# Attention sort: GpSimd makes the smaller keys of the last step of each sort place

## The reference

```python
q_prime = relu(einsum('bhld,hdm->bhlm', q, proj))
k_prime = relu(einsum('bhld,hdm->bhlm', k, proj))
kv_cumsum = cumsum(einsum('bhlm,bhld->bhlmd', k_prime, v), axis=2)
context = einsum('bhlm,bhlmd->bhld', q_prime, kv_cumsum)
norm = einsum('bhlm,bhlm->bhl', q_prime, cumsum(k_prime, axis=2))
out = (context / (norm[..., None] + 1e-06)) @ out_w + out_b
...
router_scores = softmax(xt @ Wr + br, axis=-1)          # 4096 tokens x 64 experts
order = argsort(-router_scores, axis=0)
sorted_vals = take_along_axis(router_scores, order, axis=0)
group_score = sorted_vals.reshape(Tq, G, En).sum(axis=1)
```

## Time and profile before

| | us |
|---|---|
| median of 3 runs (968.47 to 975.49) | 969.58 |
| the profiled execution | 975.05 |
| its span | 973.3 |
| DVE busy in the span | 734.6 (75%) |
| PE busy | 811.6 (83%) |
| ACT busy | 442.0 (45%) |
| POOL busy | 210.5 (22%) |

### The profile page before, as it was taken

One profiled execution on the slowest core, in us unless ns is written; L12 is line 12 of the kernel. 1 busy time (PEld: TensorE's weight loads), 2 busy tenths in 40 slices (PEclk: granted clock), 3 DMA queues, 4 the chain that ended last, 5 costly groups with the idle time before them and its releaser, 6 DMA issues. The chain is left out here.

```text
span 973.3 us, 26710 instructions
## 1 busy us (share of the span) xinstructions
PE 811.6 (83%) x10846; PEld 460.9 (47%) x10846; DVE 734.6 (75%) x1384; ACT 442.0 (45%) x785; POOL 210.5 (22%) x174
## 2 busy tenths in 40 slices
PE   6588989989887747889988969999996986689985
PEld 3366766767675512334433423433442663355542
DVE  4625545888999969999786866888885457699984
ACT  3555656656655515556677812111112355323321
POOL 7050010100100120000016843433331000224240
PEclk9679999999999968999998999999998899899998
DMA  7400000000000003566838498888781000000001
GB/s 187 100 20 4 5 4 4 4 4 4 4 4 3 4 1 151 224 241 248 280 150 352 168 351 271 281 264 269 259 280 55 1 1 1 1 11 12 23 11 33
DMA packets 49700, 104.43 MB, mean 107 GB/s; under 512 B 9968, under 2 KB 24112, under 8 KB 49456
## 3 DMA queue, kind: packets, MB, share of 16 engines
q1 hardware_dynamic: 45360, 100.68, 29.9%
q10 hardware_dynamic: 4224, 2.10, 0.8%
HBM read 53.48 MB, written 48.23 MB: 105 GB/s over the span
## 5 line engine op out<-in xcount | busy, mean ns | idle before, releaser
L1308 PE MATMUL bank<-RS,Wd 128*128 128x512 f32 x256 | 132.2, 604 | 10.1 <-DVE RS L1371 9.5
L1371 DVE TENSOR_TENSOR RS<-so_ug,bank 128x512 f32<-128x512 f32 x128 | 84.2, 672 | 24.3 <-PE bank L1294 13.2
L974 ACT ACTIVATE att_qk<-bank 128x512 f32<-128x512 f32 x128 | 66.8, 602 | 56.0 <-PE bank L744 56.0
L1273 POOL TENSOR_TENSOR so_ug<-so_ug 128x512 f32<-128x512 f32 x48 | 63.0, 1313 | 108.9 <-DMA so_ug<-hidden 108.9
L1308 PEld LDWEIGHTS bank<-RS,Wd 128*128 128x128 f32 x256 | 46.7, 191 | 62.0 <-DVE RS L1371 31.7
L1614 POOL TENSOR_TENSOR so_made<-so_ug 128x512 f32<-128x512 f32 x23 | 35.6, 1563 | 160.4 <-DVE bank L1817 150.3
L1638 ACT ACTIVATE so_ug<-bank,bu 128x512 f32<-128x512 f32 x80 | 54.7, 683 | 18.5 <-PE bank L57 18.4
L1069 DVE TENSOR_TENSOR att_am<-bank,causal 128x512 f32<-128x512 f32 x32 | 22.0, 688 | 46.1 <-PE bank L781 46.1
L55 PE MATMUL bank<-Hhi,Wgh 128*128 128x512 f16 x128 | 49.4, 386 | 8.8 <-DVE so_made L1769 8.5
L1985 POOL TENSOR_TENSOR ff_xn_h<-ff_xn_h,la_qT 128x1408 f32<-128x1408 f32 x7 | 22.2, 3169 | 153.5 <-DVE ff_xn_h L99 153.5
L481 DVE TENSOR_TENSOR att_sorting<-att_sorting 128x256 f32<-128x256 f32 x103 | 49.8, 484 | 0.0
(11 more groups left out here) (421 smaller groups left out, 1932.1 us busy)
## 6 DMA issues: line engine op xcount, KB each, us to landing
so_ug<-hidden SPq DMA_DIRECT2D x48, 768.0 KB, 4.5
hidden<-so_off SPq DMA_DIRECT2D x48, 512.0 KB, 2.9
hidden<-so_made SPq DMA_DIRECT2D x80, 256.0 KB, 2.0
so_ug<-hidden SPq DMA_DIRECT2D x16, 512.0 KB, 4.2
prep_xin<-in_L_attn_x_dram ACTq DMA_DIRECT2D x8, 256.0 KB, 7.7
out_dram<-ff_ot SPq DMA_DIRECT2D x8, 256.0 KB, 2.2
so_other<-so_key SPq DMA_DIRECT2D x2, 512.0 KB, 5.6
prep_wm<-in_L_wmod_dram SPq DMA_DIRECT2D x2, 384.0 KB, 5.9
```

The lines of the kernel that those rows point to most:

```text
L974: nc.scalar.activation(qk[t % 2][:, r, :, :].rearrange("p a l -> p (a l)"), psF[r], ACT.Relu).then_inc(s_["fe"], 1)
L1273: nc.gpsimd.tensor_tensor(u, u, g, ALU.mult).then_inc(s_pp, 1)
L1308: nc.tensor.matmul(psY[j][:, :], Wd[:, n, :], hh[n % 4][:], start=False, stop=n == EBLK - 1).then_inc(s_dn[n % 4], 1)
L1371: nc.vector.tensor_tensor(hh[i][:], pg[four % 2][:, i if four % 2 else i // 2 * 3 + i % 2, :], psW[k % 4][:, :], ALU.mult).then_inc(s_hh[k ...
```

## The change

In each sort place whose last step is a plain one (not the first step of the sort, and not one that reads the second half backwards), VectorE keeps the `max` and no longer issues the `min`. GpSimd reads both input halves as int32, adds them into a new tile `att_both`, and then subtracts the larger keys that VectorE wrote: sum less larger is the smaller. The bits of the positive floats are taken as integers for that. The list `SHARED` holds these places: 43 of the 51 in chunks 13 to 26 and 29 to 31. The next sort step on VectorE now waits for GpSimd's subtraction (it does the step's increment of the `sort` semaphore), and the subtraction waits for VectorE's `max` (`greater`) and for GpSimd's own sum (`both`). On GpSimd the sort work is put between the router's and the residual's instructions in the order of VectorE's places.

```diff
+                if i == 0 and before is not None:
+                    dve.wait_ge(before, FIRST + len(SORT_LOCAL))
...
+                if greater is not None and i == last - 1:
+                    size = SORT_LOCAL[i][0]
+                    nc.vector.tensor_tensor(halves(dst, size)[0], *halves(src, size), ALU.max).then_inc(greater, 1)
+                else:
+                    compare_exchange(dst, src, *SORT_LOCAL[i]).then_inc(stepped, 1)
...
+                SHARED = []
+                for t, (a, first, n) in sorted(SORTS.items()):
+                    cut = [0, n // 4, n * 5 // 8, n]
+                    for part in range(3):
+                        i = first + cut[part + 1] - 1
+                        if cut[part + 1] > cut[part] and i > 0 and not SORT_LOCAL[i][1]:
+                            SHARED.append((t, part, a, i))
...
-                        for s in range(NU - 1):
-                            residual(s)
-                            rt.modulate(pool, s, s, ops=nc.gpsimd)
-                            rt.h_low(pool, s, s, ops=nc.gpsimd)
+                        def lesser(t, part):
...
+                                    pool.wait_ge(s_[f"sort{a}"], FIRST + i)
+                                    nc.gpsimd.tensor_tensor(total, first.bitcast(I32), second.bitcast(I32),
+                                                            ALU.add).then_inc(s_["both"], 1)
+                                    pool.wait_ge(s_["both"], FIRST + k + 1)
+                                    pool.wait_ge(s_["greater"], FIRST + k + 1)
+                                    nc.gpsimd.tensor_tensor(lower.bitcast(I32), total, upper.bitcast(I32),
+                                                            ALU.subtract).then_inc(s_[f"sort{a}"], 1)
+                        for t in range(4, NCH):
+                            s, ph = t // 4 - 1, t % 4
+                            if ph == 3:
+                                rt.modulate(pool, s, s, ops=nc.gpsimd)
+                            lesser(t, 0)
+                            if ph == 3:
+                                rt.h_low(pool, s, s, ops=nc.gpsimd)
+                            lesser(t, 1)
+                            if ph == 1:
+                                residual(s)
+                            lesser(t, 2)
```

More of the change, by code:

```diff
@@ L9 @@
 U32 = mybir.dt.uint32
+I32 = mybir.dt.int32
 ALU = mybir.AluOpType
@@ L484, in program, with sort_tiles, halves, sort_local @@
         HELD = 19
-        def sort_local(dve, a, stepped, base, pads, scores_in, first, last):
+        def sort_tiles(a, i, pads):
             held = HELD if a == 2 else None
             own = slice(a * SORTED_RUN, (a + 1) * SORTED_RUN)
+            src = RS[:, own] if i == 0 else keys[:, own] if i == held else pads[(i + 1) % 2][:]
+            dst = keys[:, own] if i + 1 in (len(SORT_LOCAL), held) else pads[i % 2][:]
+            return dst, src
+        def halves(tile, size):
+            h = tile.rearrange("p (n k) -> p n k", k=size)
+            return h[:, :, 0:size // 2], h[:, :, size // 2:size]
+        def sort_local(dve, a, stepped, base, pads, scores_in, first, last, greater=None, before=None):
             for i in range(first, last):
@@ L494, in sort_local @@
                 dve.wait_ge(stepped, base + i)
-                src = RS[:, own] if i == 0 else keys[:, own] if i == held else pads[(i + 1) % 2][:]
-                dst = keys[:, own] if i + 1 in (len(SORT_LOCAL), held) else pads[i % 2][:]
-                compare_exchange(dst, src, *SORT_LOCAL[i]).then_inc(stepped, 1)
+                if i == 0 and before is not None:
+                    dve.wait_ge(before, FIRST + len(SORT_LOCAL))
+                dst, src = sort_tiles(a, i, pads)
+                if greater is not None and i == last - 1:
[3 more added lines that the diff above has]
+                    compare_exchange(dst, src, *SORT_LOCAL[i]).then_inc(stepped, 1)
         class Router:
@@ L660, in causal_attention @@
                 names = ("f", "fe", "kt", "kte", "S0", "S1", "Sv0", "Sv1", "Ae", "Ao", "me", "mo", "O", "Od", "To", "den",
-                         "rd", "o2", "C", "cd", "Y", "yd", "xu", "qk", "qke", "v", "vd", "sort0", "sort1", "sort2",
+                         "rd", "o2", "C", "cd", "Y", "yd", "xu", "qk", "qke", "v", "vd", "sort0", "sort1", "sort2", "greater", "both",
                          "mg", "gates", "w1T", "w1", "wq", "wqd", "gu", "dn", "pw")
@@ L681, in causal_attention @@
                 MERGES = {27: (0, 5), 28: (5, 5)}
+                SHARED = []
[5 more added lines that the diff above has]
+                            SHARED.append((t, part, a, i))
+                both = tmp.enter_context(nc.sbuf_tensor("att_both", [P, SORTED_RUN // 2], I32))
                 stand(dma=list(s_load.values()))
@@ L713, in residual @@
                             nc.gpsimd.tensor_tensor(XT[:, cols], XT[:, cols], yt[:], ALU.add).then_inc(s_["xu"], 1)
-                        for s in range(NU - 1):
-                            residual(s)
-                            rt.modulate(pool, s, s, ops=nc.gpsimd)
-                            rt.h_low(pool, s, s, ops=nc.gpsimd)
+                        def lesser(t, part):
+                            for k, (at, p, a, i) in enumerate(SHARED):
+                                if (at, p) == (t, part):
+                                    dst, src = sort_tiles(a, i, pads)
+                                    size = SORT_LOCAL[i][0]
+                                    first, second = halves(src, size)
+                                    upper, lower = halves(dst, size)
+                                    total = both[:].rearrange("p (n k) -> p n k", k=size // 2)
+                                    pool.wait_ge(s_[f"sort{a}"], FIRST + i)
[16 more added lines that the diff above has]
+                            lesser(t, 2)
                     @block.tensor
@@ L1107, in sort @@
                                 sort_local(dve, a, s_[f"sort{a}"], FIRST, pads, (rt.done(2 * a + 1, "td"),),
-                                           first + cut[part], first + cut[part + 1])
+                                           first + cut[part], first + cut[part + 1],
+                                           s_["greater"] if any(x[:2] == (t, part) for x in SHARED) else None,
+                                           s_[f"sort{a - 1}"] if a > 0 else None)
                             if t in MERGES:
```

## The result

| | us |
|---|---|
| before, median of 20 runs (960.98 to 975.49) | 969.77 |
| changed, median of 20 runs (969.87 to 978.62) | 974.03 |
| ratio, with its 95% interval | 1.0055 (1.0035 to 1.0075) |
| the profiled execution of the changed kernel | 969.87 |
| its span | 967.9 |

The change costs time, 5.3 us by the ratio (3.4 to 7.3), which is under 1% and still clear of the spread of the runs. What the 43 `min` instructions less give back is smaller than what the new waits cost.

What follows compares the result with a forecast made beforehand. VectorE was taken to set the pace of nearly every chunk with sort work. Places +2.0, +12.3 and -2.8, TensorE slack -2.8 and GpSimd order +1.3 made +10.0 on the 969.58 us median: 979.6 us, range 969 to 1000.

Steps and rivals of the forecast that it cites:

- the wait sits in slack: Rival: GpSimd at 0.62 us and more chunks than 14 and 18 waiting for TensorE; +3, 973 us; chance 0.18.
- The size of GpSimd's instruction: Each of 86 GpSimd 128x256 int32 instructions: 0.73 us, from float32 add rows; bounds 0.62, 0.85 and 1.27 us.
- The new wait: From lone `max` to next sort step: `max`, sum behind it, 0.15 us, subtraction, 0.03 us; 1.91 us unless covered.
- The second places: Second sort place of a chunk, 15 shared: +12.3 us, of it +10.2 in nine with nothing behind them.
- The port: VectorE and GpSimd share an exclusive SBUF port lock, so the sum runs behind `max`; without it, some 3.5 us less.
- First places: First sort place of a chunk, 13 shared: +0.54 us in seven covered only by the division; together +2.0 us.
- Third places and slack: Third sort place, 15 shared: eleven gain 0.25 us, -2.8; slack behind TensorE in chunks 14 and 18, another -2.8.
- it is faster: Rival: GpSimd's pair wholly hidden, 14.6 us go less some 3 in chunks that TensorE bounds; 958 us; chance 0.04.
- GpSimd's order: Sort work queued behind residual and `h_low` on GpSimd: +1.3 us, a sixth of such a row in some seven places.

Runs made afterwards that it cites:

- second pair of traces: Kernel before and changed kernel, both unchanged, run once more for a second trace: 972.10 us and 971.22 us, one run each.
- GpSimd beside whole steps: Against the kernel before: VectorE makes whole steps, GpSimd its 86 instructions on unrelated tiles, no sort step waiting: 987.47 us, ratio 1.0224.
- a second `min`: Kernel before plus one more `min` of the same input, into a tile nobody reads, in the same 43 places: 980.44 us, ratio 1.0131.
- the free removal: The 43 `min` left out with nothing in their place, GpSimd making no smaller keys, against the kernel before: 965.65 us, ratio 0.9969.

## Why the prediction was right, and which of its terms were not

The forecast was 979.6 us, +10.0, with a range of 969 to 1000; measured are 974.03 us, +5.3 by the ratio (3.4 to 7.3). That is inside the range, on the side forecast but under the 1%, and at the lower edge of the band that the forecast gave itself (+5 to +17), two thirds of the way to the rival *the wait sits in slack* (+3). The forecast held slower by over 1% for a little likelier (0.51) than within 1% (0.45), and it came within; that a change under 1% can't be told from none did not hold with 20 runs of each kernel. Measured from the lone `max` to the next sort step in both traces, place by place, the sums are:

| places | forecast | from the traces | second pair of traces |
|---|---|---|---|
| first | +2.0 | +1.2 | +0.7 |
| second | +12.3 | +10.3 | +10.3 |
| third, with the wait for TensorE behind them | -2.8 - 2.8 | -7.4 | -6.3 |
| all | +8.7 | +4.1 | +4.7 |
| everything else in the stage | +1.3 | +1.4 | +1.5 |

(The third place of chunk 31 is left out, since its next sort step lies in another stage.)

- **The size of GpSimd's instruction** was right: 0.73 us worked out of the two float32 rows, 0.72 to 0.75 us in 41 of 43 subtractions, so neither the 0.62 nor the 0.85 of its bounds.
- **The new wait** was the mis-sized term: 1.91 us forecast, 1.75 or 1.85 measured. 0.15 us to the subtraction was taken from a row with another history; it is 0.08 in 39 of 43 places. And the sum ends 0.58 us behind the `max`, as reckoned, in one kind of place only, and 0.47 behind it where the halves are single columns or pairs. Over the nine second places with nothing in between the shorter chain makes 1.2 us, and the distance before, 0.80 us and not 0.78, another 0.1; over all second places the forecast is 2.0 us too high.
- **The second places** are what costs, as forecast: shown by the run with them alone (+7.3) and the one without them (+0.5).
- **The port** holds as forecast. That it costs time with no semaphore involved is shown by the run with GpSimd beside whole steps (+21.7).
- **First places.** Two of them (chunks 17 and 30) cost nothing, which the forecast missed. Their first place is a single step, and its input was ready well ahead: in chunk 30 because the third place of chunk 29 is not shared, in chunk 17 because VectorE waited for TensorE at `am` and at a state update (0.20 and 0.94 us). In the second trace chunk 18 does the same. The sum is then done by the time of the `max` (chunk 30, both engines):

```profile
323.36 0.73 POOL L750 TENSOR_TENSOR att_both<-att_sorting 128x256 int32<-128x256 int32 x1 [3.54 <-DVE att_sorting L482]
...
324.67 0.42 DVE L511 TENSOR_TENSOR att_sorting<-att_sorting 128x256 f32<-128x256 f32 x1
...
325.24 0.73 POOL L754 TENSOR_TENSOR att_sorting<-att_both,att_sorting 128x256 int32<-128x256 int32 x1 [1.15 <-DVE att_sorting L511]
...
326.00 0.43 DVE L481 TENSOR_TENSOR att_sorting<-att_sorting 128x256 f32<-128x256 f32 x1 [0.21 <-POOL att_sorting L754]
```

  The sum starts at 323.36, 1.3 us ahead of the lone `max`, and the next step follows 1.33 us behind it, no later than before.
- **Third places and slack.** "What VectorE gains or waits moves the end, and only chunks like 14 and 18 have slack" was the step that failed as a reading. For waits it held (a second `min` costs +12.7 of 14.6). For gains it did not: the free removal brings 3.0 of 14.6 (5.3 in its trace), since `am` then waits for TensorE in nine chunks. That no wait is seen in a chunk doesn't say how far the engine behind it is. The sum came out near the mark because it was mostly a sum of waits. It is also why the rival *it is faster*, priced at 958, was never there: with a free `min` the kernel takes 966. Of the rival *the wait sits in slack* the half with GpSimd at 0.62 us was wrong, and the half with more slack behind TensorE than in two chunks was right.
- **A misread row.** Part of that slack stood in the trace of before already. Of the seven waits of the earlier trace rows four are over 1 us and three small, not four small: besides 1.42 and 2.27 us there are 1.61 in front of chunk 13 and this one, at the end of chunk 16, which the forecast gave no slack:

```profile
206.65 0.69 DVE L1069 TENSOR_TENSOR att_am<-bank,causal 128x512 f32<-128x512 f32 x1 [1.29 <-PE bank L781]
```

  It is 0.20 us after the change (0.86 in the second trace), and the third place of chunk 16 is 0.7 us shorter (0.4 in the second trace) instead of 0.25.
- **GpSimd's order.** The +1.3 was an estimate; no row gave its sixth or its seven places. TensorE now waits longer for `h_low`, before and after:

```profile
PE bank L55 <- POOL Hlo L601: 1.0, 3, 0.4
PE bank L56 <- POOL Hlo L617: 3.3, 3, 1.6
```

  VectorE's instructions that were held at the port were longer by 6.9 us in sum before and by 9.5 after. This is worked from the durations over 0.425 (128x256) and 0.69 us (128x512). None of this was tried apart, so how it splits between the places above and the +1.4 outside them is not shown.

Still open: why the differences of the runs and of the traces' stage are up to 2 us apart (+4.3 by the medians, +5.3 by the ratio, +5.5 and +6.2 in the stage), which is within what single executions vary.

## What to carry to other kernels

Work handed to a second engine in the middle of a dependent chain costs the chain's latency there, two instructions and three hand-overs in this case, and only what the first engine has to do until it needs the result is cover; look at the barest such place, not at the average. Before you count on relief of the busiest engine, see how far the next one is behind: an absence of waits tells that it isn't slower, not how much faster it is, and a kernel that leaves the work out altogether gives the upper bound of the whole idea before it is built. Where most of the noise lies in other stages, read that bound from the stage in the trace and not from the median alone.

## What the runs showed of the hardware

- GpSimd adds and subtracts int32 at the price of float32: the 128x256 sum in 0.72 to 0.73 us undisturbed, the subtraction in 0.72 to 0.75, and the float32 subtraction of the run without the sum in 0.72 to 0.74 where the halves are longer than pairs.
- Its sum was faster where the halves are single columns or pairs next to each other (last sort steps of size 2 and 4): 0.61 us undisturbed, where others take 0.72.

```profile
333.33 0.61 POOL L750 TENSOR_TENSOR att_both<-att_sorting 128x256 int32<-128x256 int32 x1
```

  Behind a `max` the same difference shows as an end 0.47 instead of 0.58 us behind it. The subtraction has no such gain (0.73 to 0.75), and the float32 one that reads one such half took longer, 0.84 to 0.86 us.
- Hand-overs in the sort: 0.08 us from the end of VectorE's `min` to GpSimd's sum, and from the sum's end to the subtraction; 0.14 us from the end of VectorE's lone `max` to the subtraction where that comes last (the run without the sum; chunks 17 and 30 of the changed kernel); 0.03 us from GpSimd's end to VectorE.
- A 128x256 VectorE instruction with two SBUF inputs that is issued while GpSimd's two-input instruction holds the port ends 0.27 to 0.29 us behind that one. In the run with GpSimd beside whole steps the tiles are unrelated, and it is the same.
